# Mixture-of-experts part of a fused layer: experts pipelined one step deeper

## What is computed

```
xn = layernorm(x)
q, k, v = heads of xn @ wq.T, wk.T, wv.T            # 16 heads of 16
y = ((q @ k.T) * SCALE * decay * causal) @ v         # per head, decay = gamma_h ** |i - j|
attn = (layernorm(y) * ln_w + ln_b) * silu(xn @ wg.T) @ wo.T
top_vals, top_idx = top_k(xn @ router_w.T + router_b, 4)       # 32 experts
rw = softmax(top_vals) * 1.8
routed = sum over the 4 of rw * down_e(silu(gate_e(xn)) * up_e(xn))    # hidden width 192
shared = shared_down(silu(shared_gate(xn)) * shared_up(xn))
out = x + attn + routed + shared
```

## Time and profile before

| | |
|---|---|
| device time, median of 3 (lowest to highest) | 202.49 us (202.48 to 203.08) |
| the profiled execution, first to last instruction | 233.7 us |
| mean granted TensorE clock in it | 0.942 |
| PE busy | 206.8 us, 89% |
| POOL busy | 112.4 us, 48% |
| packets of the 72 gathers and scatters | 3456, so 48 each |

### The profile page before, as it was taken

The page is one execution under the profiler, slowest core; times in us unless marked ns, Lnnn a source line. Parts: engine busy times, 40 slices in busy tenths (PEclk is TensorE's granted clock), DMA queues, the critical chain, the costliest instruction groups (busy, mean ns, idle before and its releaser), DMA issues.

```text
span 233.7 us, 4585 instructions
## 1 busy us (share of the span) xinstructions
PE 206.8 (89%) x1592; PEld 150.7 (64%) x1592; DVE 118.0 (50%) x359; ACT 97.0 (42%) x242; POOL 112.4 (48%) x156
## 2 busy tenths in 40 slices
PE   8999999999889799969997598929885799999995
PEld 3677667667576498839776276616655377567764
DVE  4676898998875386313342222302051223332895
ACT  2335474478943146032481337223551473105310
POOL 3150376088847757735657263754556133451000
PEclk9999999999999899985999679997999589999999
DMA  5966999930004999954422232222213023314983
GB/s 160 385 259 243 405 438 393 452 168 3 0 4 117 394 309 399 384 198 145 146 69 89 67 108 66 75 96 84 91 45 101 15 77 114 138 67 147 368 318 112
DMA packets 14855, 42.36 MB, mean 181 GB/s; under 512 B 2661, under 2 KB 6122, under 8 KB 14064
## 3 DMA queue, kind: packets, MB, share of 16 engines
q1 hardware_dynamic: 10944, 33.03, 38.1%
q0 software_dynamic: 3456, 8.92, 11.4%
q10 hardware_dynamic: 432, 0.12, 0.2%
HBM read 34.71 MB, written 7.86 MB: 182 GB/s over the span
## 4 chain that ended last, share of the span: by engine, by line
PE 65%; DVE 9%; issue 8%; another core or an unknown queue 6%; ACT 6%; DMA 4%; POOL 2%; ACTq 0%; DVEq 0%; POOLq 0%
PE bank L1564 16%; PE bank L1577 6%; PE bank L1770 5%; PE bank L1581 4%; PE bank L1434 4%; PE bank L1444 4%; PE bank L1542 3%; DMA y_rows<-y_mem,codes 3%; PE bank L1530 3%; PE bank L1601 3%; PE bank L1504 2%; PE bank L1798 2%; DVE w_mem L1100 2%; PE bank L1459 2%
## 5 line engine op out<-in xcount | busy, mean ns | idle before, releaser
L835 POOL DMA_INDIRECT y_rows<-y_mem,codes x36 | 36.2, 1007 | 48.9 <-DVE y_mem L1163 39.1
L1564 PE MATMUL bank<-xb_mem,w_mem 128*128 128x128 f32 x384 | 51.9, 289 | 3.4 <-DVE h_mem L1157 2.1
L1564 PEld LDWEIGHTS bank<-xb_mem,w_mem 128*128 128x128 f32 x384 | 48.9, 204 | 5.4 <-issue 5.3
L827 POOL DMA_INDIRECT xg_mem<-xn_rows,codes x36 | 35.4, 983 | 12.9 <-issue 10.2
L1155 DVE TENSOR_TENSOR h_mem<-h_mem,bank 128x128 f32<-128x128 f32 x32 | 9.2, 287 | 62.7 <-ACT h_mem L638 46.8
L637 ACT ACTIVATE h_mem<-bank 128x128 f32<-128x128 f32 x32 | 8.9, 278 | 40.7 <-PE bank L1564 20.7
L1163 DVE COPY y_mem<-bank 128x256 f32<-128x256 f32 x36 | 14.3, 422 | 18.3 <-PE bank L1581 14.4
L1100 DVE TENSOR_TENSOR w_mem<-bank,w_mem 128x512 f32<-128x512 f32 x32 | 20.1, 683 | 2.8 <-PE bank L1459 2.8
L1577 PE MATMUL bank<-w_mem,h_mem 128*128 128x256 f32 x60 | 19.0, 445 | 0.5 <-DVE y_mem L1163 0.5
L627 ACT COPY xb_mem<-bank 128x512 f32<-128x512 f32 x16 | 9.3, 584 | 20.7 <-remote 10.1
L650 ACT COPY w_mem<-w_mem 128x1024 f32 x16 | 16.0, 1044 | 3.5 <-PE bank L1619 2.0
(11 more groups left out here) (167 smaller groups left out, 333.7 us busy)
## 6 DMA issues: line engine op xcount, KB each, us to landing
w_mem<-w_exp_dram SPq DMA_DIRECT2D x3, 3456.0 KB, 21.9
w_mem<-w_late_dram SPq DMA_DIRECT2D x7, 1152.0 KB, 6.8
w_mem<-y_rows SPq DMA_DIRECT2D x8, 512.0 KB, 6.8
w_mem<-w_qkvg_dram SPq DMA_DIRECT2D x2, 512.0 KB, 5.8
w_mem<-decay_dram SPq DMA_DIRECT2D x1, 1024.0 KB, 7.8
xn_rows<-w_mem SPq DMA_DIRECT2D x2, 512.0 KB, 3.2
xnt_rows<-w_mem SPq DMA_DIRECT2D x1, 1024.0 KB, 4.9
w_mem<-w_ovf_dram SPq DMA_DIRECT2D x16, 64.0 KB
```

The costliest lines, as they stand in the source:

```text
L827: nc.gpsimd.indirect_dma_start(xg[:, k % RING, :], None, xn_rows, bass.IndirectOffsetOnAxis(ap=codes[:, c, 0:1], axis=0),).then_inc(tok_in ...
L835: nc.gpsimd.indirect_dma_start(y_rows, bass.IndirectOffsetOnAxis(ap=codes[:, c, 1:2], axis=0), ysb[:, k % YRING, :], None, bounds_check=RO ...
L1564: last = nc.tensor.matmul(ps_gu[j][:, m * P:(m + 1) * P], w[:, o:o + P], xbT[:, p % 2, (2 * g + j) * P:(2 * g + j + 1) * P], start=(g == 0 ...
```

## The change

Constants: `DEPTH` = 2, `UNITS` = 3, `AHEAD` = 8, `O_BASE` = (3, 6, 9, 12). The pipeline has one step more between gate-up and down, and one more between transposes and gate-up:

- On PE an ordinary step s is now: transpose pair s + 2, both gate-ups, `down(s - 2)`.
- Gate-ups use three PSUM banks, `xbT` three places (the third lies over constants that the attention has done with), the hidden values of a pair three places.
- All overflow work shares one bank, `ps_o`. Tokens are transposed at the end of step base, gate and up run at the end of base + 1, the hidden transposes at the end of base + 2, and down at the start of base + 3. The four weight copies on ACT move behind `gate_unit(2s + 1)` of step base (three) and into step base + 1 (one).
- `down(p)` signals once for both experts, `dn_ps` counts pairs.
- POOL issues gathers 8 to 15 before it takes turns, then `gather(k + 16)`, `scatter(k)`.
- At the end `down(13)` and `down(14)` follow each other, then `shared_gate_up(0)`, and only then `down_one` for the last pair.

```diff
-O_BASE = (4, 7, 10, 12)
+O_BASE = (3, 6, 9, 12)
+DEPTH = 2
+UNITS = 3
-AHEAD = 4
+AHEAD = 8
...
-        ps_xt, ps_gu, ps_dn, ps_og, ps_ot = [ps_qk, ps_vg], [ps_s0, ps_s1], [ps_sg, ps_tr], ps_y, ps_po
-        ps_sa, ps_sc, ps_sd = ps_xt, ps_gu, [ps_dn, [ps_og, ps_ot]]
+        ps_xt, ps_gu, ps_dn, ps_o = [ps_qk, ps_vg], [ps_s0, ps_s1, ps_sg], [ps_tr, ps_y], ps_po
+        ps_ot = ps_o[:, KT * P:2 * KT * P]
+        ps_sa, ps_sc, ps_sd = ps_xt, [ps_sg, ps_s0], [ps_tr, ps_y, ps_po, ps_s1]
...
 (ACT)
-                    when = [(base - 1, 1), (base, 0), (base, 0), (base, 1)] if b in (1, 2) else ...
+                    when = [(base, 1)] * (SUBS - 1) + [(base + 1, 0)]
...
 (PE, gate_up)
-                need(pe, h_sb, 2 * (n - 1))
+                need(pe, h_sb, 2 * (n - UNITS + 1))
...
 (PE, expert_step)
-                if 0 < s < PAIRS - 1:
-                    transpose_pair(s + 1)
+                if s - 3 in O_BASE:
+                    down_overflow(O_BASE.index(s - 3))
+                if 2 <= s < PAIRS - DEPTH:
+                    transpose_pair(s + DEPTH)
                 if s == 1:
                     project_out(NT - 3)
-                if 0 < s < PAIRS:
+                if s > 0:
                     gate_up(2 * s)
                 if s == 1:
+                    transpose_pair(3)
                     transpose_back(NT - 2)
                 if s == 2:
-                    project_out(NT - 1)
...
+                    transpose_back(NT - 1)
+                gate_up(2 * s + 1)
                 if s == 0:
                     transpose_back(NT - 3)
+                    transpose_pair(2)
...
+                if s >= DEPTH:
+                    down(s - DEPTH)
                 if s in O_BASE:
                     overflow_tokens(O_BASE.index(s))
                 if s - 1 in O_BASE:
                     gate_up_overflow(O_BASE.index(s - 1))
+                if s - 2 in O_BASE:
+                    transpose_hidden(O_BASE.index(s - 2))
...
-            for s in range(PAIRS + 1):
+            for s in range(PAIRS):
                 expert_step(s)
+            down(PAIRS - DEPTH)
...
             shared_gate_up(0)
+            down_one(PAIRS - 1, 0)
+            down_one(PAIRS - 1, 1)
```

More of the change, by code:

```diff
@@ L117, in token_blocks @@
 def token_blocks():
-    seq = [("P", 0), ("P", 1)]
+    seq = [("P", n) for n in range(2 * DEPTH)]
     for p in range(PAIRS):
-        if p + 1 < PAIRS:
-            seq += [("P", 2 * p + 2), ("P", 2 * p + 3)]
+        if p + DEPTH < PAIRS:
+            seq += [("P", 2 * (p + DEPTH)), ("P", 2 * (p + DEPTH) + 1)]
         if p in O_BASE:
@@ L130, in result_order @@
     seq = []
-    for s in range(1, PAIRS + 1):
-        pair, o = [("P", 2 * s - 2), ("P", 2 * s - 1)], [("O", O_BASE.index(s - 2))] if s - 2 in O_BASE else []
-        seq += o + pair
+    for s in range(DEPTH, PAIRS + DEPTH):
+        p = s - DEPTH
+        o = [("O", O_BASE.index(s - 3))] if s - 3 in O_BASE else []
+        seq += o + [("P", 2 * p), ("P", 2 * p + 1)]
     return seq
@@ L1188, in expert_step @@
                     gate_output(NT - 1)
-                if s == 2:
-                    add_residual(NT - 1)
-                if s == PAIRS - 1:
-                    results(s - 1)
                 if s < PAIRS:
@@ L1196, in expert_step @@
                     add_residual(NT - 2)
-                if s - 2 in O_BASE:
-                    overflow_result(O_BASE.index(s - 2))
+                if s == 2:
+                    add_residual(NT - 1)
+                if s >= DEPTH:
+                    results(s - DEPTH)
                 if s - 1 in O_BASE:
@@ L1201, in expert_step @@
                     multiply_overflow(oh_sb)
-                if 1 <= s and s != PAIRS - 1:
-                    results(s - 1)
             for t in range(NT):
@@ L1262, in _ @@
                     one_hot_positions(1)
-            for s in range(PAIRS + 1):
+            for s in range(PAIRS + DEPTH):
                 expert_step(s)
@@ L1600, in overflow_gate_up @@
                         o = j * OW + g * MB
-                        last = nc.tensor.matmul(ps_og[rows, 0:MB], xbO[:, g * P + SUB * j:g * P + SUB * (j + 1)],
+                        last = nc.tensor.matmul(ps_o[rows, 0:MB], xbO[:, g * P + SUB * j:g * P + SUB * (j + 1)],
                                                 o_mem[:, o:o + MB], start=(g == 0), stop=(g == KT - 1),
@@ L1614, in overflow_down @@
                     rows = slice(SUB * j, SUB * (j + 1))
-                    nc.tensor.matmul(ps_og[rows, 0:D], hTO[:, SUB * j:SUB * (j + 1)],
+                    nc.tensor.matmul(ps_o[rows, 0:D], hTO[:, SUB * j:SUB * (j + 1)],
                                      o_mem[:, j * OW + KT * MB:j * OW + XW], start=True, stop=False, skip_group_check=True)
@@ L1618, in overflow_down @@
                     rows = slice(SUB * j, SUB * (j + 1))
-                    last = nc.tensor.matmul(ps_og[rows, 0:D], hTO[I2:P, P + SUB * j:P + SUB * (j + 1)],
+                    last = nc.tensor.matmul(ps_o[rows, 0:D], hTO[I2:P, P + SUB * j:P + SUB * (j + 1)],
                                             o_mem[I2:P, j * OW + XW:(j + 1) * OW], start=False, stop=True,
@@ L1786, in shared_down @@
                     rows, routed = slice(j * I2, (j + 1) * I2), 2 * i + j in PE_TILES
-                    last = nc.tensor.matmul(to[j][:, 0:D], hSC[rows, i % 2, :], ws_mem[rows, XW:SW],
+                    last = nc.tensor.matmul(shared_bank(2 * i + j), hSC[rows, i % 2, :], ws_mem[rows, XW:SW],
                                             start=False, stop=not routed)
@@ L1797, in weigh_routed @@
                 for i, k in rows:
-                    last = nc.tensor.matmul(ps_sd[n // 2 % 2][n % 2][:, 0:D], diag[:, i, :], back[:, n, k, :],
+                    last = nc.tensor.matmul(shared_bank(n), diag[:, i, :], back[:, n, k, :],
                                             start=False, stop=(k == TOPK - 1 or (i, k) == rows[-1]))
```

179 lines of the change are left out of this document (89 added, 90 removed).

## The result

The changed kernel takes 214.47 us in the median of four runs (212.36 to 215.42), the kernel before 202.79 (202.48 to 203.95) on the same chip: slower by 5.5%, ratio 1.055 (95% interval 1.049 to 1.061). The forecast was 208.6 us, with a range of 201.5 to 212.0. The direction is right, the time is missed by 5.9 us and lies outside the range, even above the 213.9 us that all high ends together gave.

A forecast was written before the change was run, and what follows sets the result against it. The prediction took PE to bound the kernel and summed 202.5 + 4.2 (start) + 1.8 (overflow) + 0.1 (end of the experts) + 1.3 (tail) - 1.3 (gain) = 208.6 us, with a range of 201.5 to 212.0.

The forecast's parts named there:

- start: Before the transposes of pairs 3 and 4: PE waits for gathers needed a step earlier, +4.2 us, bounds 3.0 and 6.3.
- overflow downs: Before each of four overflow downs: PE waits 0.45 us for ACT's copy of the hidden transposes, +1.8 us in all.
- gain of the middle: Expert steps: waits of 0.96 and 1.16 us for hidden values and small hand-overs between gate-ups go, -1.3 us.
- end of the experts: Before down(14): PE waits 0.85 us for DVE's copies of down(13), earlier waits of 0.53 and 0.23 go, +0.1 us.
- tail: After the last down: 2.7 us of shared gate-up moved out, tail shrinks by 1.4 at the most, +1.3 us.
- What bounds the kernel: Whole kernel: bound by PE; a deeper pipeline can take away only 1.3 to 2.9 us, added waits count in full.
- The first wait: At the start, before the transposes of blocks 6 and 7: PE waits 0.7 us for gather 7.
- The second wait: At the start, before the transposes of blocks 8 and 9: PE waits 2.3 us for gather 9.
- The first rival: At the start: two pauses bring the granted clock to 0.50, 2.5 us more, 211.1 us; chance 0.14.
- The second rival: At the start: gathers land as fast as later ones, 2.5 us after issue, 205.4 us; chance 0.17.
- The fourth rival: Whole kernel: the start's pauses are there before as well and the rest cancels, 202.5 us; chance 0.06.
- The third rival: POOL's scatters were the bound: four gathers fewer between them save time, faster at 200.9 us; chance 0.13.

The follow-up runs named there:

- second profile: The kernel before, unchanged, profiled again: 202.79 us, span 200.9 us, the clock at 1.0 throughout.
- the filled wait: Changed kernel with five more matmuls, results unused, in PE's wait for the last shared hidden values: 212.28 us, ratio 1.046 to the kernel before.
- the last experiment: Against everything put back but the deeper middle: pair 3 transposed behind step 2's first gate-up, block 0's weight copies together; 201.84 us, 0.9946 to the kernel before.

## Why the prediction was right or wrong

The span's 12.7 us, by the steps of the prediction. "Measured" is read from the two profiles.

| step | forecast | measured | from |
|---|---|---|---|
| start | +4.2 | +4.9 | waits 3.34, low clock 1.64 (1.20 + 0.44) |
| copies at the first overflow block | 0 | +0.5 | L1617 waits for L663 |
| overflow downs | +1.8 | +1.8 | four waits of 0.46 |
| gain of the middle | -1.3 | -0.9 | what is left at the last gate-up, below |
| end of the experts | +0.1 | +0.9 | wait 0.95, and the rest of the way to the last down |
| tail | +1.3 | +5.5 | 25.3 us for 22.5, and 2.7 moved out |

The last expert gate-up ends 176.93 - 173.67 = 3.26 us later, with two downs (2 x 1.50 us) still to come, so PE is 6.3 us late there: 4.9 + 0.5 + 1.8 - 0.9. Then 0.9 and 5.5 are added. The gain is what is left over, so it carries the errors of the others: the kernel before has 0.17 us of the start's waits too, and the profile after is already 0.38 us late at 67 us (67.19 for 66.81), ahead of the experts. The gain may be 1.3 us as well as 0.9.

**What bounds the kernel: right.** PE is the path. That the timed runs have no standstills was right too. But the sum 18.7 + 12.5 = 31.2 us came out even by luck: it set a span (233.7) beside a timed run (202.49), which is 1.8 to 1.9 us longer than its span. The second profile's span is 200.9 us, 32.8 less, and PE is busy for 192.4 us in it, not 194.3. The forecast doesn't suffer from this, since it adds to 202.49.

**The start: mechanism right, size near, and one thing behind it not seen.** The first wait is 2.93 us, not 0.7. PE comes 2.5 us earlier than in the first trace (88.39 for 90.90), POOL's issue of gather 7 only 1.4 us (85.61 for 87.05), and PE's transposes follow the issue by 5.7 us, not by 4.5. The second wait did not come, because PE was slow in between. The first rival (the clock falls) is thus half true: 1.64 us of low clock stand where I had the second wait, and do not come on top of it. In the run with the end's order put back the clock stayed up, and the waits were 0.40, 3.10 and 1.26 us, nearly as much in all. The second rival (gathers land fast) is refuted by the changed kernel, and the run with the loads held shows what it would have taken. The fourth rival (nothing reaches the end) is refuted by the time. What I missed is the weight copy, which waits for the last late load at 105.3 us. I read the move of the copies in the diff as a move on ACT alone, and did not ask what the first of them waits for, one step earlier. In the changed kernel it costs 0.5 us; with the early transposes put back it costs 3.7 to 4.3.

**The overflow downs: right**, in place, releaser and size.

**The tail: this is the step that failed.** "The tail shrinks by 1.4 us at the most where 2.7 were moved out: +1.3 us." It did not shrink, it grew from 22.5 to 25.3 us (186.15 to 211.44). One part of that sum was near: the first routed rows came 8.5 us after the last down, where I had 8.0. But I set PE's rest (19.8 us) beside DVE's chain (21.1 us) and took the longer. In the trace they are in series: the last shared hidden values stand on DVE behind routed rows, and PE's last 6.3 us of work stand behind those. 8.5 us, 6.9 on DVE until the hidden values (194.67 to 201.57) and 6.7 on PE and DVE after it are 22.1 us at the full clock. The other 3.1 us are the clock, which the wait of 2.22 us let fall (2.2 us in the median of timed runs, as the filled wait shows). So of the 4.2 us by which the tail is longer than my 21.1, later rows make 0.5, the series 0.5 and the clock 3.1. My own sum, 21.1 us beside 19.8 us of work, had PE waiting there for 1.3 us, and I put at nothing what a wait does to the clock; I had weighed that as a rival for the start only. The Trainium skill (TensorE: Matmul & The Clock Gate, section "HAM oscillation — how this bites in real kernels"), which describes a kernel whose waits for a DMA between groups of matmuls bring the slow clock back each time, was cited there; the trace agrees with it in the changed kernel, at the start and in the tail, but not each time: the run named above had a wait of 3.10 us and a granted clock of 1.00 behind it.

The order of the shared gate-up costs 3.1 us by itself (3.7 by the medians), measured in the kernel before; the forecast had 1.3 for it. I had not asked what the pipeline's depth does at the end: two pairs' results more come behind the last gate-up, and the last scatter is 10.6 us behind it instead of 4.0. Which of the two put more into the 5.5 us is not decided. With both put back the tail takes what it took, and 5.3 us are gone.

**The end of the experts: mis-sized by 0.8 us.** The wait before `down(14)` is 0.95, as forecast (0.85). But of the waits of 0.53 and 0.23 us that I subtracted the second profile has only 0.24, and the downs themselves take somewhat longer around the wait (1.10 for 0.87 us).

**The gain: near in size, wrong in source.** The waits of 0.96 and 1.16 us are not in the second profile. What the deeper middle gains, 0.9 us by the sum and 1.1 us in the last experiment, must lie in small gaps between matmuls. The traces show a part of it: three middle steps with one overflow block take PE 17.68 us before (120.68 to 138.36) and 17.49 us in the kernel of the last experiment (119.25 to 136.74), with no wait listed in either. Where the rest lies stays open.

**The third rival (scatters are the bound, faster): refuted,** by the time and by the waits. If POOL were the bound, DVE would wait for places of `y_mem`. It does so once before the change, for 0.4 us, and never in the changed kernel. What POOL's scatters do set is when the tail gets its rows.

## What to carry to other kernels

Making a pipeline deeper can cost more at its two ends than it gives in the middle: here 4.9 us at the start and 5.3 at the end (the shared gate-up's place included) stood against about 1. Ask what the first stage needs a step earlier (every wait of it, also one that is now hidden behind another), and what follows the last stage later. Where the engine that bounds the kernel gets a wait of 2 to 3 us in a tail, price the clock behind it too. A wait taken away may only show the next one: here two late transfers lay side by side, and going round the one alone brought nothing (the other alone was not tried).

## What the runs showed of the hardware

- The same pause of PE does not always bring the same clock. Nine kernels wait 2.1 to 2.2 us for the last shared hidden values; the low clock behind it cost 3.1 us in the profile of the changed kernel, 1.6 in six others, and nothing in two. At the start a pause of 2.93 us was followed by it in the changed kernel, and so were pauses of 2.95 to 3.16 us in four other runs, but not one of 3.10 us in the run with the end's order put back. With five matmuls in the pause the clock stayed at full. Such a cost needs several runs to be told.
- A gather of 128 rows used 3.0 us after its issue with free DMA engines took 5.7 us beside bulk weight loads.
- One profiled execution of a kernel had a span of 233.7 us, and the next, of the same kernel, 200.9 us, in step with the timed runs; two of the waits on which I built were in the first alone.
